# One addition moved from GpSimd to VectorE, statistics and a reciprocal set back, and one weight split set behind the next tile's halves

## What is computed

```python
mod = (_silu(L0_c) @ L0_wmod).reshape(L0_c.shape[0], 6, 1, -1)      # sa, ca, ga, sb, cb, gb
h = _layernorm(x, axis=-1) * (1 + ca) + sa
x = x + ga * _L0_attn_ref(h, ...)
h = _layernorm(x, axis=-1) * (1 + cb) + sb
x = x + gb * _L0_ffn_ref(h, ...)
```

```python
sigma_q = elu_plus_one(q)
a_unnorm = jnp.einsum('bhsd,nhde->nbhse', sigma_q, memories)
norm = jnp.einsum('bhsd,nhd->nbhs', sigma_q, memory_norms)
a = a_unnorm / jnp.clip(norm, EPS, None)[..., None]
combined = jnp.einsum('nbhse,hn->bhse', a, weights)
out = combined.transpose(0, 2, 1, 3).reshape(b, s, HID) @ Wo.T
```

```python
h = jax.nn.silu(x @ w_gate) * (x @ w_up)
out = _sparsify_2to4(h) @ w_down
```

## Time and profile before

| | |
|---|---|
| median of 3 executions | 1367.31 us (1366.39 to 1367.68) |
| profiled execution | 1366.45 us, its span 1364.6 us |
| TensorE busy | 1341.1 us, 98% of the span |
| VectorE, ScalarE, GpSimd busy | 847.0, 637.8, 564.3 us |
| chain that ended last | TensorE 86%, VectorE 8%, ScalarE 2%, GpSimd 1% |
| granted TensorE clock | 0.999 of full speed |

### The profile page before, as it was taken

One profiled execution on the slowest core, in us unless ns is written; L12 is line 12 of the kernel. 1 busy time (PEld: TensorE's weight loads), 2 busy tenths in 40 slices (PEclk: granted clock), 3 DMA queues, 4 the chain that ended last, 5 costly groups with the idle time before them and its releaser, 6 DMA issues.

```text
span 1364.6 us, 18637 instructions
## 1 busy us (share of the span) xinstructions
PE 1341.1 (98%) x6726; PEld 1098.6 (81%) x6726; DVE 847.0 (62%) x1220; ACT 637.8 (47%) x933; POOL 564.3 (41%) x428
## 2 busy tenths in 40 slices
PE   7899999999999999999999999999999999999998
PEld 6777777777788888888888888888888888888887
DVE  6878888886746364645555575765555646363646
ACT  6677777787543343434343444433333333343321
POOL 2877777770733141414141456543232323231412
PEclk9999999999999999999999999999999999999999
DMA  6422222136202020202030322322020202020102
GB/s 256 155 93 93 92 92 81 73 93 222 79 16 85 15 85 15 85 15 85 27 88 31 100 89 89 110 68 85 15 85 15 85 15 85 15 85 15 69 0 100
DMA packets 91422, 102.43 MB, mean 75 GB/s; under 512 B 68960, under 2 KB 69504, under 8 KB 84864
## 3 DMA queue, kind: packets, MB, share of 16 engines
q1 hardware_dynamic: 91392, 102.05, 23.0%
HBM read 51.69 MB, written 33.57 MB: 62 GB/s over the span
## 4 chain that ended last, share of the span: by engine, by line
PE 86%; DVE 8%; ACT 2%; issue 2%; POOL 1%; DMA 1%; SPq 0%; DVEq 0%; ACTq 0%; POOLq 0%
PE bank L1252 27%; PE bank L1254 27%; PE bank L1253 27%; DVE banks_r L1065 3%; PE bank L1327 2%; PE bank L1339 1%; DVE inv_norm L1053 1%; POOL h_lo L457 1%; PE bank L1280 1%; DMA wmod_sb<-in_wmod_dram 1%; PE bank L1303 1%; DVE ln_raw L889 0%; DVE h_abs L1198 0%; DVE combT_lo L1030 0%; DVE xn L985 0%
## 5 line engine op out<-in xcount | busy, mean ns | idle before, releaser
L1157 DVE TENSOR_TENSOR h_act<-bank,silu_g 128x512 f32<-128x512 f32 x128 | 88.3, 690 | 411.8 <-PE bank L1254 385.7
L506 POOL TENSOR_TENSOR hs_lo<-h_abs,hs_hi 128x512 fp32r<-128x512 f32 x124 | 170.0, 1401 | 381.4 <-ACT hs_hi L774 381.4
L774 ACT ACTIVATE hs_hi<-h_abs 128x512 fp32r<-128x512 f32 x124 | 72.7, 627 | 323.7 <-DVE h_abs L1198 200.8
L457 POOL TENSOR_TENSOR h_lo<-h_raw,h_hi 128x512 fp32r<-128x512 f32 x62 | 122.2, 1999 | 233.2 <-ACT h_hi L757 233.2
L1252 PE MATMUL bank<-h_hi,gate_w_hi 128*128 128x512 f32 x512 | 199.7, 390 | 1.8 <-POOL h_lo L457 1.5
L1252 PE MATMUL bank<-h_hi,up_w_hi 128*128 128x512 f32 x512 | 199.5, 390 | 0.7 <-DVE h_act L1157 0.7
L1253 PE MATMUL bank<-h_lo,gate_w_hi 128*128 128x512 f32 x512 | 199.2, 389 | 0.0
L1253 PE MATMUL bank<-h_lo,up_w_hi 128*128 128x512 f32 x512 | 199.2, 389 | 0.0
L1254 PE MATMUL bank<-h_hi,up_w_lo 128*128 128x512 f32 x512 | 199.2, 389 | 0.0
L1254 PE MATMUL bank<-h_hi,gate_w_lo 128*128 128x512 f32 x512 | 199.2, 389 | 0.0
L1252 PE MATMUL bank<-down_w_hi,hs_hi 128*128 128x512 f32 x496 | 192.9, 389 | 0.0
(11 more groups left out here) (149 smaller groups left out, 2472.7 us busy)
## 6 DMA issues: line engine op xcount, KB each, us to landing
x_ring<-in_x_dram SPq DMA_DIRECT2D x8, 1024.0 KB, 4.9
x_scratch<-x_ring SPq DMA_DIRECT2D x8, 1024.0 KB, 3.9
xn_bits_scratch<-set_up_stage SPq DMA_DIRECT2D x8, 1024.0 KB, 4.5
over_x<-x_scratch SPq DMA_DIRECT2D x8, 1024.0 KB, 4.9
acc_scratch<-over_x SPq DMA_DIRECT2D x8, 1024.0 KB, 3.9
over_x<-acc_scratch SPq DMA_DIRECT2D x8, 1024.0 KB, 4.9
out_dram<-over_x SPq DMA_DIRECT2D x7, 1024.0 KB, 3.9
w_raw<-in_w_gate_dram SPq DMA_DIRECT2D x4, 1024.0 KB, 6.0
```

The source lines that it names most:

```text
L457: nc.gpsimd.tensor_tensor(h2_lo[:, k], h2_raw[:, k], h2_hi[:, k].bitcast(F32), ALU.subtract).then_inc(h2_lo_done, 1)
L506: nc.gpsimd.tensor_tensor(hs_lo[:, j], h_abs[:, j], hs_hi[:, j].bitcast(F32), ALU.subtract).then_inc(hs_lo_done, 1)
L774: nc.scalar.activation(hs_hi[:, j], h_abs[:, j], ACT.Copy).then_inc(hs_hi_done, 1)
L1157: nc.vector.tensor_tensor(h_act[:, cc, j], bank[2 * (j % 2) + 1][:], silu_g[:, j % 2], ALU.mult).then_inc(h_done, 1)
```

## The change

Two things are changed. In the attention phase the half sum of the second half of subtile 0's blocks, one GpSimd instruction a tile, becomes a VectorE instruction right behind the four `scale_banks` instructions of subtile 0; GpSimd waits for it with a new semaphore. The statistics of the tile before's subtile 2 (`late_stats`), which stood at that place, go behind `scale_banks` of subtile 2, next to those of subtile 3, and `combT_low` of subtile 0 changes places with the reciprocal of the last two subtiles' norms. In the feed-forward phase `split_w(SPLITS[5])` goes behind the halves of tile 1: on ScalarE behind `h2_high(1)`, on GpSimd behind `h2_low(1)`.

```diff
@@ GpSimd, attention tile
                     for i in range(2):
                         blocks = slice(i * K, (i + 1) * K)
-                        pool.wait_ge(banks_r_done, 4 * u + 2 * i + 2)
-                        nc.gpsimd.tensor_tensor(r[:, blocks, 0:2], r[:, blocks, 0:2], r[:, blocks, 2:4],
-                                                ALU.add).then_inc(half_sum_done, 1)
-                        pool.wait_ge(half_sum_done, 2 * u + i + 1)
+                        if s == 0 and i == 1:
+                            pool.wait_ge(first_sum_done, t + 1)
+                        else:
+                            pool.wait_ge(banks_r_done, 4 * u + 2 * i + 2)
+                            nc.gpsimd.tensor_tensor(r[:, blocks, 0:2], r[:, blocks, 0:2], r[:, blocks, 2:4],
+                                                    ALU.add).then_inc(half_sum_done, 1)
+                            pool.wait_ge(half_sum_done, 7 * t + max(2 * s + i, 1))
@@ GpSimd, feed-forward
             hs_low(0)
+            h2_low(1)
             split_w(SPLITS[5])
-            h2_low(1)
@@ ScalarE, feed-forward
-            item(1, 1, {0: lambda: split_w(SPLITS[5]), 1: lambda: join_h2(1, 1, 2), 2: lambda: join_h2(1, 1, 3)},
-                 started=2)
+            item(1, 1, {0: lambda: join_h2(1, 1, 2), 1: lambda: join_h2(1, 1, 3)}, started=2)
             act.wait_ge(up_done, 8)
             h2_high(1)
+            split_w(SPLITS[5])
@@ VectorE
+            def half_sum(t):
+                r, blocks = summands(0), slice(K, 2 * K)
+                dve.wait_ge(banks_r_done, 16 * t + 4)
+                nc.vector.tensor_tensor(r[:, blocks, 0:2], r[:, blocks, 0:2], r[:, blocks, 2:4],
+                                        ALU.add).then_inc(first_sum_done, 1)
@@ VectorE, attention tile (the first tile calls half_sum too)
                     scale_banks(u, 0, between=next_scalars)
-                    late_stats(t - 1, 2, u - 2)
+                    half_sum(t)
 
                 invert_norms(t, 1)
                 if first:
                     next_scalars()
                 scale_banks(u + 1, 1, first)
+                combT_low(u, 0)
                 reciprocals(2)
-                if first:
-                    combT_low(u, 0)
-                else:
-                    combT_low(u, 0)
+                if not first:
                     attn_rest(t - 1, 3, u - 1, stats=False)
                 scale_banks(u + 2, 0, first)
                 if not first:
+                    late_stats(t - 1, 2, u - 2)
                     late_stats(t - 1, 3, u - 1)
```

More of the change, by code:

```diff
@@ L201, in adaln_kernel @@
             "banks_done", "banks_r_done", "half_sum_done", "comb_done"))
+        first_sum_done = sem("first_sum_done")
         combT_done, combT_hi_done, combT_lo_done = map(sem, ("combT_done", "combT_hi_done", "combT_lo_done"))
@@ L247, in w_lo_wait, with summands @@
                 eng.wait_ge(w_lo_pool, RANK[cm] + 1 - DVE_SPLITS)
+        def summands(s):
+            return banks_r[s % 2][:].rearrange("p k n c -> p (k n c)").rearrange("p (b n c) -> p b n c", n=NB, c=HALF)
         LAST_ITEM = 2 * NT2 - 1
@@ L462, in tile @@
                     u = 4 * t + s
-                    r = banks_r[s % 2][:].rearrange("p k n c -> p (k n c)").rearrange(
-                        "p (b n c) -> p b n c", n=NB, c=HALF)
+                    r = summands(s)
                     for i in range(2):
                         blocks = slice(i * K, (i + 1) * K)
-                        pool.wait_ge(banks_r_done, 4 * u + 2 * i + 2)
-                        nc.gpsimd.tensor_tensor(r[:, blocks, 0:2], r[:, blocks, 0:2], r[:, blocks, 2:4],
-                                                ALU.add).then_inc(half_sum_done, 1)
-                        pool.wait_ge(half_sum_done, 2 * u + i + 1)
+                        if s == 0 and i == 1:
[5 more added lines that the diff above has]
+                            pool.wait_ge(half_sum_done, 7 * t + max(2 * s + i, 1))
                         if i == 0 and not (first and s == 0):
```

## The result

The changed kernel takes 1373.72 us (median of 5 executions, 1373.10 to 1374.55), against 1367.09 us for the kernel before (5 executions beside it): ratio 1.0049, interval 1.0037 to 1.0060. That is +6.6 us, where +4.95 had been forecast. The profiled execution took 1373.72 us with a span of 1371.9; the one of before had 1364.6, so the two traces differ by 7.3 us. One execution in experiment 1 (4769.3 us) and two of the kernel before beside it (7237.73 and 1491.75 us) were slow and are left out of the comparisons; with it counted, that kernel's median would be 1371.21 us instead of 1371.06, which is the +4.1 that two later expectations use.

The account below looks back on a forecast made before the run. TensorE was taken to bound the kernel nearly everywhere. Attention +1.95 and feed-forward +3.0 us summed to +4.95: 1366.45 becomes 1371.4 for a profiled-like execution, median 1372.3 us; range 1366.0 to 1374.5.

Parts of the forecast that it names:

- The sign and the sum: Whole kernel: slower, attention +1.95 and feed-forward +3.0 us, together +4.95 us; chance of slower by more than 2.7 us, 0.61.
- the likeliest of the cases: Whole kernel: the forecast itself, both phases slower, 1370.5 to 1374 us; chance 0.55.
- The rival of no change: Feed-forward: the split's turns fall elsewhere, mask late by at most about 1.5 us; 1369.6 us or less; chance 0.26.
- the faster one: Both phases: TensorE keeps 0.45 us in seven tiles and loses both `h2_lo` waits; 4.6 us faster, 1362.7; chance 0.13.
- The half sum: Attention tiles 1 to 6: with the addition on VectorE, TensorE's 0.31 us wait goes; Wo of subtile 0 some 0.45 us earlier.
- The third rival: Attention: VectorE's addition takes 1.15 us in each tile; +7.8 us, 1375.1; chance 0.06.
- The statistics: Attention tiles 1 to 6: two BN_STATS ahead of `combT_lo` make Wo of subtile 1 0.2 us later; together +1.2 us.
- The last tile: Attention, last tile: VectorE has no gap, so the whole addition is paid, +0.75 us, ends 0 and +1.2.
- The first tile: Attention, first tile: no statistics there and VectorE waits for ScalarE later; 0, ends -0.45 and +0.2 us.
- The planes: Feed-forward, ScalarE: planes land at 355.7, so 1.6 of the 1.8 us freed are waited; +0.15 us, both `h2_lo` waits stay.
- The mask beside the split: Feed-forward: GpSimd's split beside item 1's mask makes it 4.0 us later; TensorE stalls 2.85 us for tile 1's silu.
- The slack of 1.15: Feed-forward: tile 1's first silu was ready 1.15 us before TensorE's third gate block, at 380.39, needed it.

Follow-up runs that it names:

- experiment 1: Two kernels, each the kernel before with part of the change: feed-forward edits alone, 1371.06 us; attention edits alone, 1368.52 us.
- experiment 4: Kernel before with the weight split late on both engines (GpSimd's behind `hs_low(1)`), and the transposing DMA issued ahead of the down weight's load: 1365.68 us.
- experiment 2: Feed-forward edits alone, with 0, 2 or 3 of GpSimd's four split pieces ahead of `hs_low(1)`, the rest behind: 1367.49, 1367.97, 1369.42 us.
- the kernels with 3 and 4 pieces: Kernel before with feed-forward edits alone, three or all four of GpSimd's split pieces ahead of item 1's mask: 1369.42 and 1371.06 us.
- experiment 5: Subtile 2's statistics moved into VectorE's wait ahead of the norms: with the attention edits alone, 1365.12 us; in the kernel before, without VectorE's addition, 1367.34 us.

## Why the prediction was right, and where its sizes were off

**The sign and the sum.** Forecast +4.95, measured +6.6, inside the range; the likeliest of the cases happened. The rival of no change and the faster one fell to the same row: the wait of 2.76 us for `silu_g`.

**The half sum.** The places in tile 6 came out within 0.1 us: transposes without a wait, Wo of subtile 0 at 259.70 (259.6 or 259.7 forecast), the next scalings at 258.59 - 2.34 = 256.25 (256.11 + 0.15 forecast). One reason given did not: VectorE's addition was to wait for GpSimd's half sum until 254.75. It started at 256.95 - 2.34 = 254.61, with GpSimd's record running on to 257.09 - 2.34 = 254.75, and took 0.69. It stands 0.12 behind the place of the statistics, which I read as its wait for the scalings to land, and nothing was added by GpSimd. That GpSimd was held up is borne out: the first of its two `combined`, which started beside the addition, took 1.07, and the second 0.72. The third rival, an addition of 1.15, is out.

**The statistics.** The forecast was a lead of 0.45 given back and 0.2 lost; measured are 0.35 and 0.17 in tile 6, and 0.15 a tile over the six. The last tile cost 0.43 where the whole addition, 0.75, was taken: part of it still had cover there. In medians the attention is +1.4 (experiment 1), forecast +1.95.

**The first tile.** The sum put it at 0, with ends of -0.45 and +0.2, because it has no statistics to move. It cost 0.4, outside both ends: VectorE has no gap there to take the addition (the rows below the ledger). That the attention still came out near its forecast in the trace, 0.4 + 0.9 + 0.4 = 1.7 where 0 + 1.2 + 0.75 had been added up, is partly luck: this term was too low and the two others too high.

**The planes.** Right, and shown by experiment 4: 1.48 us of wait for the transfer on ScalarE in the changed kernel (1.46 in experiment 2's), where 1.6 was forecast, and the two waits for `h_lo` stay.

**The mask beside the split.** Forecast 4.0 us late and a stall of 2.85; the trace has 6.16 - 2.14 = 4.02 and a stall of 2.76. The 4.0 was read off, where the same instructions had once run beside the same split. The slack of 1.15 was a little too large: experiment 2 has 0.95 to 1.0.

**The term that was missing** is the price of the stall beyond its own length. The sum put TensorE's stall at 2.85 and let the matmuls behind it run at full speed. They ran at half clock for 3.4 us, and this stretch took another 1.8. The profile of before has such a fall too (a granted clock of 0.64 from 8 to 12 us, where TensorE had just waited 4.29 us for a DMA), so a stall of nearly 3 us should have carried a possible second price in the sum. Waits of 0.7 to 0.9 alone mostly had none: eight traces have the two waits for `h_lo` with the clock at 1.00 behind them, and it fell there in two, those of the kernels with 3 and 4 pieces. What decides it was not told apart.

**Left open.** Why the clock falls behind the waits for `h_lo` in some traces and behind silu in another; why the medians of experiment 2 rise faster than its traces; the alternating tiles of experiment 5.

## What to carry to other kernels

When an instruction moves on one engine, look at which instructions of another engine it will now run beside: here the split's own length was harmless, and what it did to four small mask instructions on VectorE, with the fall of the clock that came of it, cost 5.4 us. Where the trace of before has the same pair side by side once, read the price there: here it was right to a tenth of a microsecond. A gain at one wait is worth something only if the next wait on the same engine has slack for it, and in a tile where the engine that takes the work over has no gap, the work costs at once (0.4 us in tile 0); put what must be moved into an idle stretch of its own engine (here 1.07 us ahead of the norms) and not ahead of the next thing that TensorE needs.

## What the runs showed of the hardware

**VectorE and GpSimd side by side.** Small bf16 instructions with two SBUF inputs went from 0.43 to 1.40 us, and those on 1024 columns from 0.69 to 1.66, while GpSimd's split was running, and the split was stretched as well: 6.57 us for four pieces, 1.64 each, where the one piece that ran without the mask, in the kernel with three ahead, took 1.29. In the changed kernel the two engines go by turns. The four pieces end at 375.62, 377.05, 378.75 and 380.45, and the four slowed mask instructions end at 375.90, 377.60, 379.30 and 380.73: 0.28 us behind a piece where the instruction is one of the short ones (0.42 or 0.43 alone), 0.55 where it is one of the long ones (0.69 alone). Each of the next three pieces ends 1.15 us behind the mask instruction before it. That fits whole instructions that wait for each other; a bandwidth shared between the two would stretch them by their overlap, without such even steps. The Trainium skill, page "SBUF — State Buffer", section "SBUF: two separate sides", describes a lock that is held for a whole instruction, and these rows agree with it. In the attention phase `combined` agrees too: 1.07 us beside the addition, 0.72 behind it. The addition itself, 0.69 us long and begun 0.14 before the end of a GpSimd record, was not delayed; whether it had to wait for that instruction the rows cannot tell, because the ends of GpSimd's records are rough.

**The clock.** A fall to 0.50 lasted 3.4 us in each of the three traces that have one at the start of tile 1, and cost 1.6 us where nothing covered it and next to nothing where TensorE would have waited anyway. At the start of the program, where the instructions of all the kernels are the same, the first norms came at 34.8 to 35.0 us in four traces and at 35.6 to 36.1 in eight; in seven of these eight the granted clock was 0.58 to 0.68 from 12 to 16 us, and in the kernel before, one of the four, 0.93.
